# Cross-attention and quantised feed-forward: row-tiled scores of head pairs, mask and minimum fused on VectorE, and an order written out for each engine

## The reference

```
z  = layernorm(x)
k  = [fside @ Wk.T + bk ; ctx @ Wgk.T + bgk]      # 512 keys, 16 heads of 64
v  = [fside @ Wv.T + bv ; ctx @ Wgv.T + bgv]
q  = z @ Wq.T + bq
att = q @ k.T / 8 ; the first 256 keys of a row are -inf where the mask is true
x  = x + softmax(att) @ v @ Wo.T + bo
x  = x + fp8_gemm(layernorm(x))                    # e4m3 quantised, 256 x 256
```

## Time and profile before

| | us |
|---|---|
| median of 3 runs | 2911.33 (2909.72 to 2912.35) |
| span of the profiled execution | 2906.8 |
| median less span | 4.5 |
| PE busy | 2793.8 (96%) |
| PE weight loads | 2431.0 (84%) |
| DVE busy | 2315.1 (80%) |
| POOL busy | 2099.0 (72%) |
| ACT busy | 1982.3 (68%) |
| chain that ended last | PE 61%, DVE 17%, issue 13%, ACT 7% |

### The profile page before, as it was taken

How to read it: one execution, slowest core, us unless ns; L and a number is a source line. 1 busy time by engine, 2 the same in 40 slices (tenths; PEclk the granted TensorE clock), 3 DMA queues, 4 the chain that set the end, 5 groups by cost and what they waited for, 6 DMA issues and landing times.

```text
span 2906.8 us, 68146 instructions
## 1 busy us (share of the span) xinstructions
PE 2793.8 (96%) x20352; PEld 2431.0 (84%) x20352; DVE 2315.1 (80%) x3793; ACT 1982.3 (68%) x4742; POOL 2099.0 (72%) x2504
## 2 busy tenths in 40 slices
PE   5999999999999999999999999999999999999997
PEld 4888888888888888888888888888888888888886
DVE  5888778888778887788887788877888877888776
ACT  4666676766677666767666776667676667766674
POOL 4777777777768777777777687777777776877775
PEclk9999999999999999999999999999999999999998
DMA  5333333333333333333343333333333433333331
GB/s 170 82 77 90 76 86 82 80 79 91 72 90 87 76 90 76 87 83 79 79 92 71 90 87 76 90 77 86 85 79 78 93 69 90 87 76 90 78 82 37
DMA packets 176029, 243.02 MB, mean 84 GB/s; under 512 B 25472, under 2 KB 92544, under 8 KB 176000
## 3 DMA queue, kind: packets, MB, share of 16 engines
q1 hardware_dynamic: 176000, 242.66, 35.6%
HBM read 66.40 MB, written 8.39 MB: 26 GB/s over the span
## 4 chain that ended last, share of the span: by engine, by line
PE 61%; DVE 17%; issue 13%; ACT 7%; DMA 1%; DVEq 1%; POOL 0%; SPq 0%; ACTq 0%; POOLq 0%
PE ps_misc L555 20%; PE ps_o L658 10%; PE ps_pt L645 10%; PE ps_misc L599 8%; PE ps_scores L631 5%; PE ps_scores L632 5%; DVE pt_lo L941 5%; DVE kv_out L912 3%; PE ps_scores L634 2%; ACT probs L786 2%; DVE q_lo L889 2%; DVE scr_b L875 1%; DVE o_t L949 1%; ACT zq_out L751 1%; DVE scr_a L877 1%
## 5 line engine op out<-in xcount | busy, mean ns | idle before, releaser
L481 POOL TENSOR_SCALAR probs<-probs,recips 128x512 f32<-128x512 f32 x1024 | 698.4, 694 | 457.0 <-DVE recips L936 456.8
L795 ACT CAST pt_hi<-ps_pt 128x512 fp32r<-128x512 f32 x1024 | 551.7, 595 | 319.8 <-PE ps_pt L645 314.5
L786 ACT ACTIVATE probs<-ps_scores,neg_max 128x512 f32<-128x512 f32 x1024 | 696.0, 688 | 23.5 <-DVE neg_max L932 11.4
L941 DVE TENSOR_TENSOR pt_lo<-ps_pt,pt_hi 128x512 fp32r<-128x512 f32 x1024 | 655.2, 680 | 53.2 <-ACT pt_hi L795 50.3
L932 DVE TENSOR_REDUCE neg_max<-ps_scores 128x2 f32<-128x1024 f32 x512 | 621.1, 1213 | 9.5 <-PE ps_scores L634 9.5
L658 PE MATMUL ps_o<-pt_hi,v_hl 128*128 128x256 f32 x2048 | 554.6, 302 | 1.0 <-DVE o_t L949 1.0
L645 PE MATMUL ps_pt<-ident,probs 128*128 128x128 f32 x4096 | 531.5, 273 | 1.6 <-DVE pt_lo L941 1.6
L658 PE MATMUL ps_o<-pt_lo,v_hl 128*128 128x256 f32 x2048 | 511.4, 281 | 0.0
L645 PEld LDWEIGHTS ps_pt<-ident,probs 128*128 128x128 f32 x4096 | 464.5, 141 | 8.6 <-POOL probs L481 2.0
L631 PE MATMUL ps_scores<-k_hl,q_hh 128*128 128x512 f32 x1024 | 456.8, 446 | 9.0 <-issue 4.7
L632 PE MATMUL ps_scores<-k_hl,q_lo 128*128 128x512 f32 x1024 | 407.1, 398 | 0.0
(11 more groups left out here) (106 smaller groups left out, 6567.1 us busy)
## 6 DMA issues: line engine op xcount, KB each, us to landing
k_hl<-k_split SPq DMA_DIRECT2D x1024, 128.0 KB, 2.3
mask_sb<-mask_dram SPq DMA_DIRECT2D x128, 256.0 KB, 3.3
q_hh<-q_hh SPq DMA_DIRECT2D x256, 128.0 KB, 2.4
x_sb<-x_dram SPq DMA_DIRECT2D x32, 256.0 KB, 2.8
side_raw<-side_t_dram SPq DMA_DIRECT2D x32, 256.0 KB, 3.6
scr_b<-ctx_t_dram SPq DMA_DIRECT2D x32, 256.0 KB, 2.8
out_dram<-y SPq DMA_DIRECT2D x32, 256.0 KB, 2.1
probs<-wq_t_dram SPq DMA_DIRECT2D x1, 1024.0 KB, 5.1
```

The source lines that it names most:

```text
L481: nc.gpsimd.tensor_scalar(probs[:, h % 2, t, :], probs[:, h % 2, t, :], recips[:, h % 2, t:t + 1], 1.0, ALU.mult, ALU.mult).then_inc(norm_ ...
L786: nc.scalar.activation(probs[:, h % 2, t, :], ps_scores[:, h % 2, t, :], ACT.Exp, bias=neg_max[:, h % 2, t:t + 1], scale=-1.0, accum_out=s ...
L795: nc.scalar.copy(pt_hi[:, h % 2, 2 * k:2 * k + 2, :], ps_pt[:, k, :, :]).then_inc(pthi_done, 1)
L941: V.tensor_tensor(pt_lo[:, h % 2, 2 * k:2 * k + 2, :], ps_pt[:, k, :, :], pt_hi[:, h % 2, 2 * k:2 * k + 2, :].bitcast(F32), ALU.subtract). ...
```

## The change

1. **Scores of a pair.** q_hi, q_lo, k_hi and k_lo are kept as they come from the projection: the even head of a pair on partitions 0-63, the odd one on 64-127. For each half t of the queries, three products of 64 contraction rows are made for each of the two heads, alternating, into the two banks that `ps_scores` now has. `place_keys` and `place_queries`, `k_hl`, `q_hh`, `k_split` and `zq_out` are gone.
2. **Mask and minimum.** The mask product is gone. One VectorE operation for each head and half reads the bank and the mask bytes (and a row of zeros for the second 256 keys), adds them, scales by 2^80 (taken out of Wq), writes `probs` and accumulates the minimum. `exps` then works in place in `probs`.
3. **Rings and banks.** `probs`, `neg_max`, `sums` and `recips` have 4 places, `kv_out` 4, `ps_o` and `ps_misc` 2 banks each. `ps_scores` falls from 4 banks to 2.
4. **q and z** are split straight from PSUM: ScalarE writes the high part, VectorE the rest.
5. **Order.** `PLACES` is replaced by one list of calls for each engine, for a whole batch. The six quantising steps are single calls. The order of the chunks is unchanged.

```diff
-                if free:
-                    pe.wait_ge(exp_done, QT * (g - 1))
-                for t in range(QT):
-                    dst = ps_scores[:, h % 2, t, :]
-                    rows = slice(t * P, (t + 1) * P)
-                    mm(dst, q_hh[:, n % 2, i, rows], k_hl[:, n % 2, i, :], start=True, stop=False)
-                    mm(dst, q_lo[:, n % 2, i, rows], k_hl[:, n % 2, i, :], start=False, stop=False)
-                    m = mask_sb[:, n % 2, (i * QT + t) * S:(i * QT + t + 1) * S].bitcast(FP8E5)
-                    last = mm(dst[:, 0:S], mask_weight[:], m, start=False, stop=True)
+                if some(c.head(h) + t):
+                    pe.wait_ge(min_done, 2 * (c.head(h) + t))
+                rows = slice(t * P, (t + 1) * P)
+                for i, (q, k) in enumerate(((q_hi, k_hi), (q_lo, k_hi), (q_hi, k_lo))):
+                    for e in range(2):
+                        own = slice(e * DK, (e + 1) * DK)
+                        last = mm(ps_scores[:, e, :], q[own, n % 2, a, rows], k[own, n % 2, a, :],
+                                  start=(i == 0), stop=(i == 2))
                 last.then_inc(scores_done, 1)
...
-            def mins(h, g):
-                dve.wait_ge(scores_done, g + 1)
-                V.tensor_reduce(neg_max[:, h % 2, :], ps_scores[:, h % 2, :, :], AX_X, ALU.min).then_inc(min_done, 1)
+            def mins(c, h, t):
...
+                    if some(g + 2 - RING):
+                        wait_apart(dve, "dve", pt_full, 2 * (g + 2 - RING))
+                if h % 2 == 0:
+                    wait_apart(dve, "dve", scores_done, g + t + 1)
+                row = (h // GH % 2 * GH + h % GH) * QT + t
+                s = ps_scores[:, h % 2, :].rearrange("p (k s) -> p k s", s=S)
+                p = probs[:, h % RING, t, :].rearrange("p (k s) -> p k s", s=S)
+                V.tensor_tensor_reduce(out=p, in0=s, in1=mask_sb[:, row::MASK_ROWS - row, :], scale=MASK_STEP,
+                                       scalar=SCORE_LIMIT, op0=ALU.add, op1=ALU.min,
+                                       accum_out=neg_max[:, h % RING, t:t + 1]).then_inc(min_done, 1)
...
+            def split_los(c, kind, n):
...
+                for cols, hi, lo, bias in split_parts(kind, n):
+                    src = ps_misc[:, bank, cols]
+                    if bias is None:
+                        last = V.tensor_tensor(lo, src, hi.bitcast(F32), ALU.subtract)
+                    else:
+                        last = V.scalar_tensor_tensor(out=lo, in0=src, scalar=bias, in1=hi.bitcast(F32),
+                                                      op0=ALU.add, op1=ALU.subtract)
```

The start of TensorE's written order, as an example of the lists (`scores(c, h, t)` is the pair h, h + 1):

```diff
+            def batch(c):
+                chunk(c, "k0", 1)
+                scores(c, 2, 0)
+                outputs(c, -1)
+                transposes(c, 0, 0)
+                transposes(c, 0, 1)
+                scores(c, 2, 1)
+                chunk(c, "q", 1)
+                transposes(c, 1, 0)
+                transposes(c, 1, 1)
+                outputs(c, 0)
+                chunk(c, "wo0_prev", 0)
+                chunk(c, "k1", 1)
+                transposes(c, 2, 0)
+                transposes(c, 2, 1)
+                scores(c, 4, 0)
+                chunk(c, "wo1_prev", 0)
+                scores(c, 4, 1)
...
```

More of the change, by code:

```diff
@@ L27 @@
 BF16 = mybir.dt.bfloat16
-FP8E5 = mybir.dt.float8e5
 U8 = mybir.dt.uint8
@@ L54 @@
 E4_OVERFLOW = 1.69e33
-PLACES = {
[6 rows of a table removed]
[L66 to L72, removed]
+CHUNKS = [
[5 rows of a table added]
+]
 PROLOGUE = [("zt_next", 0), ("q", 0), ("k0", 0), ("v0", 0), ("k1", 0), ("v1", 0)]
@@ L75 @@
 PREV = WO + ("xq_prev", "ff_prev")
[L78 to L91, removed]
 K_KINDS = ("k0", "k1")
@@ L93 @@
 V_KINDS = ("v0", "v1")
[L94 to L114, removed]
@@ L117 @@
[L117 to L133, removed]
+KV = K_KINDS + V_KINDS
@@ L556, in split_product, with chunk @@
                 return last
-            def chunk(c, place, first=False):
-                kind, n = c.at[place]
-                start = c.before(place)
-                pe.wait_ge(misc_free, start)
+            def chunk(c, kind, n):
+                if (kind, n) not in c.chunks:
+                    return
                 if kind == "q" and n == 0:
-                    pe.wait_ge(zq_ready, c.before(place, ZQ))
+                    pe.wait_ge(misc_free[BANK["zt_next", 0]], c.through(("zt_next", 0)))
@@ new lines, in transposes @@
+            def transposes(c, h, k):
+                if k == 0:
+                    pe.wait_ge(norm_done, QT * c.head(h) + QT)
+                if some(c.head(h)):
+                    pe.wait_ge(ptlo_done, 2 * c.head(h) - 1 + k)
+                for j in range(2):
+                    for t in range(QT):
+                        kt = 2 * k + j
+                        last = nc.tensor.transpose(ps_pt[:, k, j, t * P:(t + 1) * P],
+                                                   probs[:, h % RING, t, kt * P:(kt + 1) * P], ident[:])
+                last.then_inc(pt_full, 1)
@@ L724, in _ @@
-            batch(0, first=True)
-            with pe.Fori(1, B - 1) as b:
-                batch(b)
-            batch(B - 1, last=True)
-            outputs(H - 1, H * B - 1)
-            for j, kind in enumerate(PREV):
-                pe.wait_ge(misc_free, TAIL_AT + j)
-                run_chunk(kind, 0, B).then_inc(misc_full, 1)
+            for kind, n in PROLOGUE:
+                if kind != "zt_next":
+                    pe.wait_ge(w_split, {"q": 1, "k0": 3, "k1": 3, "v0": 4, "v1": 5}[kind])
+                chunk(c, kind, n)
@@ L850, in _ @@
-            batch(0, first=True)
-            with act.Fori(1, B - 1) as b:
-                batch(b)
-            batch(B - 1, last=True)
-            o_los(H * B - 1)
-            for j, kind in enumerate(PREV):
-                if kind not in WO:
-                    chunk(kind, 0, TAIL_AT + j, 0, 0, B)
+            split_his(c, "zt_next", 0)
+            weight_hi("k")
+            weight_hi("gk")
+            act.wait_ge(consts_done, 1)
+            split_his(c, "q", 0)
+            weight_hi("v")
@@ L1054, in _ @@
-            batch(0, first=True)
-            with dve.Fori(1, B - 1) as b:
-                batch(b)
-            batch(B - 1, last=True)
-            o_adds(H - 1, H * B - 1)
-            for t, kind in enumerate(WO):
-                chunk(kind, 0, TAIL_AT + t, 0, B)
-            normalise_y(B)
-            quantise(B, 0)
-            quantise(B, 1)
+            copy_values(c, "v1", 0)
+            dve.wait_ge(mask_zeros, 1)
+            for t in range(QT):
+                mins(c, H, t)
+                mins(c, H + 1, t)
```

1230 lines of the change are left out of this document (764 added, 466 removed), and 11 rows, old and new, of tables (CHUNKS, PLACES).

## The result

The changed kernel takes 2734.64 us (median of 4 runs, 2734.26 to 2735.61) against 2910.52 before; the ratio is 0.9398, with a 95% interval from 0.9385 to 0.9411. Forecast were 2723 us and a range of 2600 to 2925.

A forecast was written before the change was run, and what follows sets the result against it. The prediction took TensorE's own work as the bound. Per batch, 77.6 us of work + 3.2 of mode changes + 2.1 of waits = 82.9; 32 periods + 66.2 + 4.5 gave 2723 us, range 2600 to 2925.

The forecast's parts named there:

- Side by side, 3 x 0.235 for a pair: Score products: two heads' half-array products overlap fully, so a pair and query half holds TensorE 0.705 us against 1.175 before.
- Mode change at 0.10: Going in and out of the pair products: 0.10 us a change, bounds 0 and 0.35, 3.2 us a batch.
- rival A: Both ends of each score group: full drain and weight load, 0.35 us a change, 2980 us in total; chance 12%.
- The drained end of 0.16: Mode change on TensorE: waiting for the last product to drain, 0.16 us, alone would give 84.8 a batch and 2784 us.
- Rival D: Mode change at score groups is free, as type and transpose changes are: 79.7 us a batch, total 2621; chance 20%.
- 2.1 us of waits: TensorE's waits per batch under the new order and banks: 2.1 us taken, bounds 1 and 6.
- the prediction's last sentence: On the period between z transposes: if it is 83 us but by other terms, the sum was luck.
- What is added to the periods: Outside the 32 batch periods: 66.2 us for weights, first heads and last feed-forward, plus 4.5 from span to median.
- Forecast were 70.5: VectorE's work per batch: from 72.3 to 70.5 us, fused operations at 0.68 each, hidden below TensorE's 80.8.
- ScalarE and GpSimd off the path: Per batch ScalarE falls from 62 to 56.4 us and GpSimd keeps 65.6, both covered by TensorE.
- The placing DMAs off the path: Removing 1024 + 256 placing DMAs from SP's queue gains nothing directly; k_hl lands 2.3 us after issue, beside other work.
- Only what shortens TensorE's own work can bring much: Kernel before: TensorE's work, 85.1 us of an 88.77 us period, is the bound; 3.7 us are lost in waits.

## Why the prediction was right, and where it was not

- **Side by side, 3 x 0.235 for a pair: right.** The pairs start together, and the third follows the second by 0.24. The 3.07x of the Trainium skill, "TensorE: Matmul & The Clock Gate", Part 3, is for four tiles; the 0.92 us that the prediction estimated from it is not seen for two, since the lost time lies at the ends and not in the overlap.
- **Mode change at 0.10: too low.** It is 0.19, twice the restart of the earlier trace rows: 6.0 us a batch, not 3.2. The bound of 0.35 was too high, and rival A's threshold of 0.284 was not reached. The drained end of 0.16 that the prediction had beside its value was the better guess. Rival D (free) is excluded by the kernel with one half-array product, 107 us above the one with none.
- **2.1 us of waits: too high.** 66.3 for the other work + 16 x 1.08 = 83.6 against a period of 83.31: nothing is left for waits (the 0.3 is the rounding of the groups' lengths). The two errors, +2.8 and -2.1 or a little more, cancel. That the forecast is only 12 us off is luck in these two terms, as the prediction's last sentence said it would be.
- **What is added to the periods: nearly right.** Outside the 32 periods lie 66.9 us (2732.8 - 32 x 83.31), for 66.2 forecast. The 4.5 from span to median came from one profiled execution before that lay under the median; after, it is 1.8 (2734.6 - 2732.8).
- **VectorE: right in kind, 2.9 us a batch too high.** Forecast were 70.5, measured 67.6 (2163.6 / 32). The fused operation came as sized, without a second pass; q_lo at 476 ns each was dearer than the 424 taken. For the rest, some other VectorE groups shrank (z from 955 to 623 ns, one quantising step from 1428 to 951) and some grew (xq from 752 to 1096), while the DMA queues moved 74.8 MB in place of 242.7; no run shows what caused either.
- **ScalarE and GpSimd off the path: right.** 58.1 and 64.0 us a batch for 56.4 and 65.6; exp from SBUF takes 725 ns for 688 from PSUM, which the prediction had put at nearly nothing.
- **The placing DMAs off the path: right for the old order.** TensorE's products waited 1.2 us for k_hl in all. In the new order as it is written, placing DMAs cost 865 us or more. This order therefore leans on their removal, a link that the prediction did not see.
- **"Only what shortens TensorE's own work can bring much": wrong as a statement on the kernel before.** In the old order 80% of what is taken from TensorE comes back as waits (24 of 123 us arrive), while the new order with the old score price gains 130 us. The period of the old kernel was TensorE's work plus those 3.7 us, but they grow as the work shrinks, at the single misc bank in the rows above. The sum came right because the change took away work and waits at once.

The division of the 172 us, then: 130 for order, banks, ring and the move of mask and minimum, which were changed together here and which no run separates in full; 42 for the score group, out of 0.47 us saved in streaming for each group less 0.375 given back at its ends (0.095 x 512 = 49). Within the 42, leaving out the mask product is worth 88 and row tiling in place of four whole-array products costs 46; what row tiling buys is that no placing DMAs are needed, and in this order those cost far more.

## What to carry to other kernels

Where an engine is 96% busy and the rest is waits for others, ask whether a microsecond taken from it arrives: take one piece out and time it. Row tiling on 64 rows pays for streaming, not for short visits: each change into or out of the half arrays cost 0.19 us, so six of 512 columns won only 0.1 us a group over four whole-array ones of 512 and two of 256, and lose 0.14 to the four alone. Groups should be long or rare. An order written out by hand holds only for the latencies and banks that it was written with: one bank less cost 1090 us, placing DMAs for each chunk 865. Read the granted clock beside such numbers: it fell to a mean of 0.939 and 0.899 in those two runs, so TensorE's own work grew as well.

## What the runs showed of the hardware that I had not expected

Products on different halves of the array start together even where the program puts two others between them, with the same total time (2734.75 against 2734.64 us). A read of VectorE's accumulator (81 ns) runs beside the next operation and adds nothing. A single 64-row product between 128-row ones costs as much in mode changes (0.18 each way) as a full pair group. SyncE issues DMAs of 60 KB some 0.64 us apart, so six for one chunk spend 3.1 us before the last is even on its way.
